# Work from behind the attention chunks moved between their steps, and the value product in quarters of the array

## The chip, the cores and the metric

The kernel runs on one core of one Trainium2 chip. The metric is the device time of one execution in microseconds. TensorE (PE), VectorE (DVE), ScalarE (ACT), GpSimd (POOL) and SyncE (SP, which here only issues transfers) run side by side and meet at semaphores.

## What is computed

```python
x = L0_attn_x                                  # 2 x 2048 tokens, 256 wide, fp32
h = _layernorm(x) * (1 + ca) + sa              # mod from silu(c) @ wmod
x = x + ga * attention(h, Wqkv, Wout)          # 16 heads of 64, causal window of 128
h = _layernorm(x) * (1 + cb) + sb
x = x + gb * experts(h)                        # 8 experts, top 2 by softmax, 640 rows
...                                            # per expert and choice; 256 -> 1024 -> 256
```

Within the window a query of a block of 128 tokens sees the keys of its own block up to itself and those of the block before that lie behind it: two triangles that together make one full block.

## The kernel before

The 4096 tokens are eight chunks of 512 (four tiles of 128); chunks 0 to 3 are the first batch. A chunk has 16 units, each half of a pair of heads (two heads, two of the four tiles); in the last chunk (7) the units run over the pairs for the first two tiles, then for the last two. `chunk` of each engine walks 16 steps, numbered 4 to 19. In step i, PE issues the scores of unit i (line 637, `scores`; from 16 on that is a unit of the next chunk), the values of unit i-4 (lines 668 and 675, `weighted_values`), the turning of unit i-2 (line 648, `transposes`), and projections of the next chunk (line 600 for queries and keys, 614 for values). DVE merges the two triangles (1109), takes maximum and reciprocal (1113, 1117) and normalises (1121); ACT takes the exponentials (909), copies the turned probabilities out of the bank `pt` (917) and empties the projections (894, 901); POOL splits the triangles into previous and own keys (`split_keys`, 1422 and 1424). The result in the one bank `pv` is written as high and low fp16 halves, by ACT (923) and DVE (1134), once per pair; in the last chunk once per unit (931, 1246).

Score and value products are fp32; each is recorded as two matmuls. Scores work in quarters of the array (64 rows, 64 columns), values in halves (128 rows of keys, 64 columns), the rest on all of it. fp16 products are three matmuls on high and low halves.

The projections write two banks in turn, `gen0` and `gen1`: `chunk_groups` lists all groups of a chunk in order, and `claim` makes PE wait until the group before the previous one has been emptied. Behind the 16 steps stand the four value tiles of the second half of the heads (`projections_after`) and the output projection of the chunk (`project_out`, 691); DVE then adds the result to `x` (`add_attention`, 1142 and 1146).

The second layernorm, the choice of experts and the sending of rows for chunk c-1 (`ROUTE_AT`) run during chunk c: statistics, then scale and shift on POOL (370, 374), packing on ACT (943), the low half on POOL (379), turning by DMA, logits on PE (740), softmax and top 2 on DVE, counts on PE (754), slots on DVE (1206 to 1227), and eight scatters on POOL (1433). SP also copies the last block of keys of each pair for the next chunk by DMA (530; in chunk 0 DVE does it, 1093), clears the slots in the first 110 us (522) and turns normalised rows (535). After chunk 7 come the experts (1603, 1617). All of `x` stays in memory (32 tiles).

```python
    LATE_PACKED = 2016
...
                names = [("qk"[i % 2], (i - LAG) // 2)] + ([("v", 0, v_tiles[i])] if i in v_tiles else [])
...
                return names + projections_after(c) + out_groups
```

## Time and profile before

| | us |
|---|---|
| median of 3 runs | 1151.61 |
| lowest, highest | 1149.98, 1154.63 |
| profiled execution, its own time | 1147.24 |
| its span (first to last instruction) | 1144.4 |
| chunk 0, start to end | 54.4 to 135.4 |
| chunks 1 to 5 | 83.3 each |
| chunks 6 and 7 | 73.7 and 71.0 |
| experts | from 707.4 |

The profiled execution took 2.8 us more than its span, and 4.4 us less than the median of the runs. Busy time of an engine in a stage, set against the stage's length, tells how far it is from setting the pace there; the mean granted TensorE clock over the span is 0.991 of full.

### The profile page before, as it was taken

The numbers are of one execution on the slowest core, as the hardware profiler recorded it, in microseconds if no ns is written. First come the engines' busy times: TensorE is split into PE (matmuls) and PEld (weight loads), VectorE is DVE, ScalarE is ACT, GpSimd is POOL, SyncE is SP. The second block draws the span as 40 slices with busy tenths as digits, with TensorE's granted clock in tenths as the row PEclk, the third lists the DMA queues.
The fourth block names the chain that finished last, engine by engine and source line by source line (L and its number), as shares of the span: only waits on it lengthen the run. The fifth ranks groups of instructions, "written<-read, shape, count | busy, mean of one in ns | idle before, by whom it ended". The sixth has DMA issues, their size and how long they took to land.

```text
span 1144.4 us, 25293 instructions
## 1 busy us (share of the span) xinstructions
PE 1084.4 (95%) x9469; PEld 711.8 (62%) x9469; DVE 750.3 (66%) x1663; ACT 660.5 (58%) x1874; POOL 506.2 (44%) x555
## 2 busy tenths in 40 slices
PE   7999999999999999999998885989999999999996
PEld 4455655655655655655656564756776858585765
DVE  5776586586576585674675784756676766666653
ACT  5677476476476476476473853447474563727461
POOL 2234274365275365355445655434344352525342
PEclk9999999999999999999999998999999999999998
DMA  9744111112021021021031024434345353534000
GB/s 335 151 163 138 40 29 48 38 37 52 27 45 48 24 46 45 24 45 39 24 103 48 5 83 121 92 94 81 109 94 153 97 112 111 112 112 78 23 20 9
DMA packets 140114, 87.41 MB, mean 76 GB/s; under 512 B 96708, under 2 KB 130650, under 8 KB 139868
## 3 DMA queue, kind: packets, MB, share of 16 engines
q1 hardware_dynamic: 129244, 64.29, 21.4%
q0 software_dynamic: 10752, 21.54, 6.6%
q8 instruction: 75, 1.23, 0.5%
q14 instruction: 43, 0.35, 0.1%
HBM read 40.02 MB, written 33.79 MB: 64 GB/s over the span
## 4 chain that ended last, share of the span: by engine, by line
PE 75%; issue 7%; DVE 7%; ACT 6%; POOL 4%; DMA 0%; SPq 0%; POOLq 0%; DVEq 0%; ACTq 0%
PE down L1617 18%; PE up L1603 17%; PE gen L600 10%; PE gen L614 7%; PE gen L691 6%; PE score L637 4%; PE pv L668 4%; PE pt L648 4%; ACT prob L909 4%; PE pv L675 3%; DVE prob L1121 2%; POOL h L370 1%; POOL probT_split L1424 1%; PE gen L699 1%; POOL probT_split L1422 1%
## 5 line engine op out<-in xcount | busy, mean ns | idle before, releaser
L1643 ACT ACTIVATE hid<-up,b1T 128x512 f16<-128x512 f32 (+2 forms) x192 | 124.3, 648 | 182.1 <-PE up L1603 180.3
L1603 PE MATMUL up<-xT,w 128*128 128x512 f16 (+2 forms) x1152 | 212.5, 346 | 10.9 <-issue 10.9
L1617 PE MATMUL down<-w,hid 128*128 128x256 f16 x1920 | 213.7, 274 | 3.2 <-DVE hid L1659 3.2
L1422 POOL TENSOR_SCALAR_AFFINE_SELECT probT_split<-probT 128x512 f32<-128x512 f32 x128 | 102.9, 804 | 250.9 <-ACT probT L917 247.4
L1617 PEld LDWEIGHTS down<-w,hid 128*128 128x128 f16 x1920 | 188.6, 98 | 27.6 <-DVE hid L1659 3.7
L600 PE MATMUL gen<-hT,big 128*128 128x512 f16 x768 | 185.0, 380 | 0.6 <-DVE hT L1371 0.6
L909 ACT ACTIVATE prob<-score,negmax 128x128 f32<-128x128 f32 x512 | 180.7, 375 | 0.7 <-DVE negmax L1113 0.7
L1603 PEld LDWEIGHTS up<-xT,w 128*128 128x128 f16 x1152 | 112.9, 98 | 104.9 <-issue 12.8
L1702 POOL DMA_INDIRECT out<-y,tail x80 | 82.4, 1031 | 206.1 <-DVE y L1687 193.2
L1659 DVE TENSOR_TENSOR hid<-hid 128x512 f16<-128x512 f32 (+2 forms) x192 | 115.2, 606 | 72.4 <-ACT hid L1644 72.0
L917 ACT ACTIVATE probT<-pt 128x512 f32<-128x512 f32 x128 | 76.9, 601 | 99.0 <-PE pt L648 98.8
L1109 DVE COPY_PREDICATED score<-above,score 128x512 f32<-128x512 int32 x112 | 77.5, 692 | 77.3 <-PE score L637 77.2
L1644 ACT ACTIVATE hid<-up,b1T 128x512 f32<-128x512 f32 (+2 forms) x192 | 124.8, 650 | 0.0
L600 PEld LDWEIGHTS gen<-hT,big 128*128 128x128 f16 x768 | 73.8, 98 | 67.7 <-issue 1.2
L637 PE MATMUL score<-k,q 64*64 64x192 f32 (+2 forms) x2048 | 111.0, 330 | 2.6 <-issue 2.2
L909 ACT ACTIVATION_READ_ACCUMULATOR prob<-score,negmax 128x1 f32 x512 | 111.0, 217 | 0.0
L1692 POOL DMA_INDIRECT kept<-out,tail x80 | 86.5, 1081 | 47.6 <-issue 30.0
L1121 DVE TENSOR_TENSOR prob<-prob,rinv 128x512 f32<-128x512 f32 x128 | 103.4, 808 | 0.0
L668 PE MATMUL pv<-probT_split,v 128*64 128x256 f32 x512 | 83.5, 403 | 19.0 <-DVE attn L1134 7.0
L637 PEld LDWEIGHTS score<-k,q 64*64 64x64 f32 x2048 | 64.5, 132 | 53.9 <-issue 51.6
L614 PE MATMUL gen<-big,hT 128*128 128x512 f16 x384 | 89.1, 379 | 2.3 <-DVE logit L1160 1.2
L1424 POOL TENSOR_SCALAR_AFFINE_SELECT probT_split<-probT 128x512 f32<-128x512 f32 x128 | 86.3, 674 | 0.0
(159 smaller groups left out, 1442.4 us busy)
## 6 DMA issues: line engine op xcount, KB each, us to landing
big<-in_L_ffn_W SPq DMA_DIRECT2D x14, 1024.0 KB, 6.9
slot_inputs<-empty_row SPq DMA_DIRECT2D x80, 129.5 KB, 2.3
out<-x SPq DMA_DIRECT2D x7, 512.0 KB, 3.3
x<-in_L_attn_x SPq DMA_DIRECT2D x1, 3072.0 KB, 22.8
k<-k SPq DMA_DIRECT2D x48, 64.0 KB, 1.9
kept<-out,tail POOLq DMA_INDIRECT x80, 3.1
out<-y,tail POOLq DMA_INDIRECT x80, 2.4
x<-in_L_attn_x SPq DMA_DIRECT2D x2, 512.0 KB, 6.9
```

What stands on the lines that cost most here:

```text
L600: mm = pe.matmul(dst[:], wqkv[:, kd, a, col:col + P], hT[:, cn % 2, kd, b, :], start=(n == 0), stop=(n == 5))
L614: mm = pe.matmul(dst[:], hT[:, cn % 2, kd, a, s * P:(s + 1) * P], wqkv[:, kd, b, 2 * INNER + half * 512:2 * INNER + (half + 1) * 512], sta ...
L637: mm = pe.matmul(dst[lo:lo + HALF, 2 * hd + i, first:lo + P + HALF], q[r:r + DH, j, b * P + lo:b * P + lo + HALF], k[r:r + DH, j, b * P + ...
L668: mm = pe.matmul(pv[r:r + DH, 2 * part * P:(2 * part + 2) * P], v[:, 2 * part + 1, h * DH:(h + 1) * DH], probT_split[:, par, 2 * hd:2 * hd ...
L909: mm = act.activation(prob[:, h % 2, b, :], score[h % 2][:, b, P:], ACT.Exp, bias=negmax[:, h % 2, b:b + 1], accum_out=rowsum[:, h % 2, b: ...
L1121: dve.tensor_tensor(prob[:, h % 2], prob[:, h % 2], rinv[:, h % 2, :].unsqueeze(2).to_broadcast([P, TILES, P]), ALU.mult)\
L1422: pool.affine_select(out=probT_split[:, h % 2, :, 1], in_=probT[:, h % 2], pattern=[[0, TILES], [1, P]], compare_op=ALU.is_ge, fill=zero, ...
L1603: mm = pe.matmul(bank, w1[:, par, kd, a, ft * P:(ft + 1) * P], part_rows(e, n, xT[:, par, b * KD + kd, :]), start=(i == 0), stop=(i == 5))
L1617: mm = pe.matmul(down[n][:, s, :], hid[:, ft, a, t * P:(t + 1) * P], w2[:, par, ft, b, :], start=(i == 0), stop=(i == 3 * FT - 1))
L1643: act.activation(part_rows(e, n, hid[:, ft, 0, :]), bank, ACT.Relu, scale=1 / W_SCALE, bias=bias).then_inc(hid_hi, 1)
L1644: act.activation(part_bank(e, n, hid32[:, k_ % 4, :]), bank, ACT.Relu, scale=1 / W_SCALE, bias=bias).then_inc(up_out, 1)
L1659: dve.tensor_tensor(part_rows(e, n, hid[:, ft, 1, :]), part_bank(e, n, hid32[:, k_ % 4, :]), part_rows(e, n, hid[:, ft, 0, :]), ALU.subtra ...
```

## The change

1. **Values in quarters.** In chunks 0 to 6 a value product is no longer made of whole blocks of 128 keys. `half_values` takes the upper 64 keys of a new unit (`high_keys`) and the lower 64 keys of the unit before it (`low_keys`), in turn, and leaves out the 64x64 corners that the window masks. The two go to two banks, `pv0` and `pv1`. The lower half of a unit comes a step later (`LO_AT` 5, `HI_AT` 4). High and low fp16 halves are written per unit, and `attn` has 24 slots of 256 columns in a ring. The last chunk keeps `weighted_values`, on two banks.
2. **The turned probabilities** lose the bank `pt`: they take their turn on `gen0` and `gen1`. ACT copies them straight into `probT_split` (three buffers, `RING`), where POOL splits them in place.
3. **The output projection** of chunk c-1 runs in steps 4, 6, 8 and 11 of chunk c, a tile at a time (`late_out`, `add_tile`), the second half of chunk c's own values in steps 5, 7, 9 and 10. Chunk 6 keeps its output behind its steps.
4. **Routing** moves: statistics to packing of chunk c-1 from steps 4 to 9 to steps 8 to 16 of chunk c, logits to sending into steps 4 to 12 of the chunk after that. The rows that chunk 6 makes ready are chosen and scattered behind its steps (`logits_late`, `counts_late`).
5. **Key copies** are DVE's in all chunks (`keep_keys`).
6. **x** has 24 tiles; chunks 6 and 7 are loaded later into places that are free by then. Expert 0's weights go to other places and are loaded after chunk 6; their splits move from steps 5 to 8 of the last chunk to 7 to 10.

```diff
-    LATE_PACKED = 2016
+    X_PLACE = (2, 3, 0, 1, 4, 5, 2, 3)
+    X_CHUNKS = max(X_PLACE) + 1
+    ATTN_SLOTS = H + PAIRS
+    LATE_PACKED = (ATTN_SLOTS - H) * 4 * P
     EARLY_TILES = 3
+    RING = 3
     EARLY_ROWS = EARLY_TILES * P
...
-            probT_split = sb("probT_split", [P, 2, TILES, 2, P], F32)
+            probT_split = sb("probT_split", [P, RING, TILES, 2, P], F32)
...
-            attn = sb("attn", [P, PAIRS, 2, CHUNK], F16)
+            attn = sb("attn", [P, ATTN_SLOTS, 2, 2 * P], F16)
...
-            pv = ps("pv", [P, CHUNK], F32)
+            pv = [ps(f"pv{i}", [P, CHUNK], F32) for i in range(2)]
...
-                v_tiles = {12: 0, 13: 1, 14: 2, 16: 3}
+                v_tiles = {13: 0, 14: 1, 16: 2, 17: 3}
...
-                return [n for n in v_half(1) if c < LAST and (c != LAST - 1 or n not in LATE_NAMES)]
...
+                return [n for n in v_half(1) if c == LAST - 1 and n not in LATE_NAMES]
...
+            OUT_TILE = {4: 0, 6: 1, 8: 2, 11: 3}
+            SECOND_V = {5: 0, 7: 1, 9: 2, 10: 3}
...
+            ROUTE_AT = {"stats": (8, 13), "rstd": 13, "norm": 14, "scale": 14, "shift": 15, "token": 16, "pack": 16, "low": 16}
+            CHOOSE_AT = {"logits": 4, "softmax": 5, "exp": 5, "top": 6, "counts": 7, "slots": 8, "send": 9, "sent": 13}
...
-            SPLIT_AT = [5, 6, 7, 8]
+            SPLIT_AT = [7, 8, 9, 10]
...
+                    names += [("pt", i)]
+                    if c > 1:
+                        names += ([("logits",)] if i == CHOOSE_AT["logits"] else []) + ([("counts",)] if i == CHOOSE_AT["counts"] else [])
...
+                        names += [("tile", OUT_TILE[i])] if i in OUT_TILE else []
+                        names += [("own v", SECOND_V[i])] if i in SECOND_V else []
+                    names += projections_at(c, i)
...
+                    def transposes(n_unit, c, name):
+                        pe.wait_ge(norm_ready, n_unit + 1)
+                        dst, full = claim(c, name)
...
+                            mm = pe.transpose(dst[:, b * P:(b + 1) * P], prob[:, n_unit % 2, b, :], identf[:])
+                        mm.then_inc(full, 1)
...
+                        at_least(pe, attn_lo, n_unit - 1)
...
+                    def high_keys(c, u, hd, i, cur):
+                        n_unit = H * c + u
+                        j, part = unit_of(c, u)
+                        r, h, b = DH * hd, 2 * j + hd, 2 * part + i
+                        first = HALF * cur
+                        return pe.matmul(pv[n_unit % 2][r:r + DH, i * P + first:(i + 1) * P], v[HALF:, b + cur, h * DH:(h + 1) * DH],
+                                         probT_split[HALF:, n_unit % RING, 2 * hd + i, cur, first:], start=(i == 0 and cur == 0),
+                                         stop=False, skip_group_check=True)
+
+                    def low_keys(c, u, hd, i, cur):
+                        n_unit = H * c + u
+                        j, part = unit_of(c, u)
+                        r, h, b = DH * hd, 2 * j + hd, 2 * part + i
+                        last = P if cur else HALF
+                        return pe.matmul(pv[n_unit % 2][r:r + DH, i * P:i * P + last], v[0:HALF, b + cur, h * DH:(h + 1) * DH],
+                                         probT_split[0:HALF, n_unit % RING, 2 * hd + i, cur, 0:last], start=False,
+                                         stop=(cur == 0), skip_group_check=True)
+
+                    def half_values(c, new, old):
+
+                        if old is not None:
+                            pe.wait_ge(high_done, H * old[0] + old[1] + 1)
+                        if new is not None:
+                            values_there(c, new)
+                        for i in range(2):
+                            for n in range(2):
+                                for hd in range(2):
+                                    if new is not None:
+                                        high = high_keys(c, new, hd, i, n)
+                                    if old is not None:
+                                        low = low_keys(*old, 1 - hd, i, 1 - n)
+                        if new is not None:
+                            high.then_inc(high_done, 1)
+                        if old is not None:
+                            low.then_inc(pv_done, 1)
...
+                    def late_out(c, t):
+                        if c == 0 and t == 0:
+                            pe.wait_ge(split_lo, 8)
+                        pe.wait_ge(attn_lo, H * c + (H - 1 if t < 2 else H))
+                        dst, full = claim(c + 1, ("tile", t))
+                        project_out_tile(c, dst[:, 0:D], t, range(PAIRS)).then_inc(full, 1)
...
+                                scores(c, i)
+                                half_values(c, i - HI_AT, (c, i - LO_AT) if i >= LO_AT else (c - 1, H - 1) if c > 0 else None)
+                            transposes(H * c + i - 2, c, ("pt", i))
+                            if c > 1 and i == CHOOSE_AT["logits"]:
+                                route_logits(c - 1)
+                            if c > 1 and i == CHOOSE_AT["counts"]:
+                                route_counts(c - 1)
+                            if c > 0 and i in OUT_TILE:
+                                late_out(c - 1, OUT_TILE[i])
+                            if c > 0 and i in SECOND_V:
+                                project_v(c - 1, 1, [SECOND_V[i]])
+                            for name in projections_at(c, i):
+                                project(c, name)
+                        if c == LAST - 1:
                             for name in projections_after(c):
                                 project(c, name)
-                            project_out(c)
-                            return
-                        pe.wait_ge(attn_lo, PAIRS * c + H - 1)
+                            route_logits(c)
+                            project_out_pair(c, 0)
+                            route_counts(c)
+                            project_out_pair(c, 1)
...
                     def copy_probT(c, h):
                         u = H * c + h
-                        act.wait_ge(pt_done, u + 1)
-                        at_least(act, prev_ready, u - 1)
-                        act.activation(probT[:, h % 2], pt[:], ACT.Copy).then_inc(probT_ready, 1)
-
-                    def attn_high(c, j):
-                        act.wait_ge(pv_done, H * c + 2 * j + 2)
-                        if j == 0:
-                            at_least(act, x2_ready, 2 * c)
-                        act.activation(attn[:, j, 0, :], pv[:], ACT.Copy).then_inc(attn_hi, 1)
+                        bank, before = turned_in(u)
+                        act.wait_ge(gen_full[bank], before + 1)
+                        at_least(act, pv_done, u - RING + 1)
+                        act.activation(probT_split[:, u % RING, :, 1], gen[bank][:].rearrange("p (a q) -> p a q", q=P), ACT.Copy)\
+                           .then_inc(gen_free[bank], 1)
 
...
+                    def keep_keys(c, j):
+
+                        dve.wait_ge(scores_done, H * c + 2 * j + 2)
+                        dve.tensor_copy(k[:, j, 0:P], k[:, j, CHUNK:]).then_inc(k_halo[j], 1)
 
...
+                    def add_tile(c, t):
+
+                        bank, before = group(c + 1, ("tile", t))
+                        if c == 0 and t == 0:
+                            dve.wait_ge(mod_spread, 16)
+                        at_least(dve, x2_ready, TILES * c + t)
+                        dve.wait_ge(gen_full[bank], before + 1)
+                        dve.scalar_tensor_tensor(gated[:, t % 2, :], gen[bank][:, 0:D], 1 / W_SCALE, modrow[:, batch(c), 0, :],
+                                                 ALU.mult, ALU.mult).then_inc(gen_free[bank], 1)
+                        dve.wait_ge(gen_free[bank], before + 1)
+                        row = x[:, x_at(c) + t, :]
+                        dve.tensor_tensor(row, row, gated[:, t % 2, :], ALU.add).then_inc(x2_ready, 1)
 
                     def route_tokens(r):
                         c, t0, nt, rows_out = route_round(r)
...
                         for i in STEPS:
-                            if i >= 6 and i % 2 == 0 and not last:
-                                attn_low(c, (i - 6) // 2)
-                            if not first and not last and i == at["softmax"]:
+                            if i > LO_AT:
+                                attn_low_part(c, i - LO_AT - 1)
+                            elif c > 0:
+                                attn_low_part(c - 1, H + i - LO_AT - 1)
+                            if c > 0 and i == LO_AT:
+                                keep_v(c - 1, 1)
+                            if c > 0 and i - 1 in OUT_TILE:
+                                add_tile(c - 1, OUT_TILE[i - 1])
+                            if c > 1 and i == CHOOSE_AT["softmax"]:
+                                route_softmax(c - 1)
+                            if c > 1 and i == CHOOSE_AT["slots"]:
+                                route_slots(c - 1)
...
+                        pool.wait_ge(gen_free[bank], before + 1)
+                        whole, own = probT_split[:, u % RING, :, 1], probT_split[:, u % RING, :, 0]
+                        pool.affine_select(out=own, in_=whole, pattern=[[0, TILES], [-1, P]],
+                                           compare_op=ALU.is_gt, fill=zero, base=0, channel_multiplier=1).then_inc(prev_ready, 1)
+                        pool.affine_select(out=whole, in_=whole, pattern=[[0, TILES], [1, P]],
                                            compare_op=ALU.is_ge, fill=zero, base=0, channel_multiplier=-1).then_inc(cur_ready, 1)
```

PE in the first step of chunk 2. Before:

```order
L637 MATMUL score0<-k,q 64x192 x8
L668 MATMUL pv<-probT_split,v 64x256 x2
L675 MATMUL pv<-probT_split,v 64x128 x4
L648 MATMUL pt<-identf,prob 128x128 x4
L600 MATMUL gen0<-hT,big 128x512 x6
```

and now, from the second half of the value product on (line 703 is `high_keys`, 712 `low_keys`, 755 an output tile, 813 the logits, 683 the turning):

```order
L703 MATMUL pv0<-probT_split,v 64x128
L712 MATMUL pv1<-probT_split,v 64x128
L703 MATMUL pv0<-probT_split,v 64x128
L712 MATMUL pv1<-probT_split,v 64x128
L703 MATMUL pv0<-probT_split,v 64x64
L712 MATMUL pv1<-probT_split,v 64x64
L703 MATMUL pv0<-probT_split,v 64x64
L712 MATMUL pv1<-probT_split,v 64x64
L683 MATMUL gen0<-identf,prob 128x128 x4
L813 MATMUL gen1<-gate16,h2T 128x8 x24
L755 MATMUL gen0<-wout,attn 128x256 x24
L636 MATMUL gen1<-hT,big 128x512 x6
```

The value product has become 16 small products between the scores and the turning, and two groups, logits and an output tile, stand between the turning and the projection. The turned probabilities and the output tile are on the same bank, `gen0`, the logits and the projection on `gen1`.

DVE in steps 9 and 10 of a middle chunk (1080 and 1180 are `ln_shift`). Before:

```order
L1109 COPY_PREDICATED score1<-above,score1 128x4x128
L1117 RECIPROCAL rinv<-rowsum 128x4
L1113 TENSOR_REDUCE negmax<-score1 128x4
L1121 TENSOR_TENSOR prob<-prob,rinv 128x512
L1080 SCALAR_TENSOR_TENSOR xn<-xn,rstd0,kept 128x256 x2
L1134 TENSOR_TENSOR attn<-pv,attn 128x512
L1109 COPY_PREDICATED score0<-above,score0 128x4x128
L1117 RECIPROCAL rinv<-rowsum 128x4
L1113 TENSOR_REDUCE negmax<-score0 128x4
L1121 TENSOR_TENSOR prob<-prob,rinv 128x512
L1080 SCALAR_TENSOR_TENSOR xn<-xn,rstd0,kept 128x256 x2
```

and now, from the first instruction of step 9:

```order
L1355 TENSOR_TENSOR attn<-pv1,attn 128x256
L1251 SCALAR_TENSOR_TENSOR gated<-gen1,modrow 128x256
L1255 TENSOR_TENSOR x<-x,gated 128x256
L1209 COPY_PREDICATED score1<-above,score1 128x4x128
L1217 RECIPROCAL rinv<-rowsum 128x4
L1213 TENSOR_REDUCE negmax<-score1 128x4
L1221 TENSOR_TENSOR prob<-prob,rinv 128x512
L1180 SCALAR_TENSOR_TENSOR xn<-xn,rstd0,kept 128x256 x2
L1355 TENSOR_TENSOR attn<-pv0,attn 128x256
L1193 COPY k<-k 128x128
L1209 COPY_PREDICATED score0<-above,score0 128x4x128
```

The low half comes in every step and for one unit, ahead of it all; behind it stand the residual of an output tile (1251, 1255) or a key copy (1193), both ahead of the merge.

POOL at the end of chunk 6. Before, the scatters stood between the pairs of selects of that chunk's last four steps:

```order
L1422 AFFINE_SELECT probT_split<-probT 128x4x128
L1424 AFFINE_SELECT probT_split<-probT 128x4x128
L1433 DMA slot_inputs<-packed,send 10240x518 x2
L1422 AFFINE_SELECT probT_split<-probT 128x4x128
L1424 AFFINE_SELECT probT_split<-probT 128x4x128
```

and now all eight stand behind the last pair, ahead of the selects of chunk 7's second unit:

```order
L1550 AFFINE_SELECT probT_split<-probT_split 128x4x128
L1552 AFFINE_SELECT probT_split<-probT_split 128x4x128
L1561 DMA slot_inputs<-packed,send 10240x518 x8
L1550 AFFINE_SELECT probT_split<-probT_split 128x4x128
L1552 AFFINE_SELECT probT_split<-probT_split 128x4x128
```

## Rows read from the trace of the kernel before

**Rows 1.** the page, part 1: busy us (share of the span) x instructions

```profile
PE 1084.4 (95%) x9469; PEld 711.8 (62%) x9469; DVE 750.3 (66%) x1663; ACT 660.5 (58%) x1874; POOL 506.2 (44%) x555
```

**Rows 2.** busy time, chunks 0, 2, 6, 7: length; PE, PEld, DVE, ACT, POOL; clock

```profile
54.40:135.40 81.00, 79.72 (x755) 48.75 (x754) 50.06 (x105) 52.37 (x186) 26.38 (x35) 1.00 0.37 120
218.70:302.00 83.30, 81.61 (x791) 50.21 (x790) 56.05 (x137) 51.36 (x179) 41.80 (x48) 1.00 0.17 40
551.90:625.60 73.70, 68.75 (x731) 44.71 (x731) 50.24 (x121) 44.81 (x168) 38.65 (x45) 1.00 0.20 62
625.60:696.60 71.00, 61.68 (x676) 41.75 (x675) 54.33 (x152) 44.85 (x147) 41.16 (x43) 1.00 0.16 53
```

**Rows 3.** PE in order of time, one plain step; start, us, what

```profile
226.15 0.88 PE L637 MATMUL score<-k,q 64*64 64x192 f32 x16
226.96 0.65 PE L668 MATMUL pv<-probT_split,v 128*64 128x256 f32 x4
227.44 0.61 PE L675 MATMUL pv<-probT_split,v 128*64 128x128 f32 x8
227.98 0.66 PE L648 MATMUL pt<-identf,prob 128*128 128x128 f32 x4
228.47 1.46 PE L600 MATMUL gen<-hT,big 128*128 128x512 f16 x6
```

**Rows 4.** what PE waited for, whole run: us, times, longest

```profile
PE pv L668 <- DVE attn L1134: 7.0, 13, 1.3
PE pv L668 <- POOL probT_split L1424: 6.9, 14, 1.4
...
PE pv L668 <- DVE attn L1246: 2.1, 2, 1.3
```

**Rows 5.** score instructions alone, the first 0.03 us of a step

```profile
222.43:222.46 0.03, 0.02 (x4) 0.03 (x4) 1.00 0.96 341
```

**Rows 6.** PE in order of time, the logits of chunk 2

```profile
251.93 0.75 PE L740 MATMUL gen<-gate,h2T 128*128 128x8 f16 x24
252.53 1.45 PE L600 MATMUL gen<-hT,big 128*128 128x512 f16 x6
```

**Rows 7.** PE in order of time, behind chunk 1

```profile
202.97 5.34 PE L614 MATMUL gen<-big,hT 128*128 128x512 f16 x24
208.15 10.64 PE L691 MATMUL gen<-wout,attn 128*128 128x256 f16 x96
```

**Rows 8.** ACT in order of time, the same plain step

```profile
228.03 0.22 ACT L909 ACTIVATION_READ_ACCUMULATOR prob<-score,negmax 128x1 f32 x1
228.68 0.60 ACT L917 ACTIVATE probT<-pt 128x512 f32<-128x512 f32 x1 [0.42 <-PE pt L648]
```

**Rows 9.** groups of instructions by line and shape: us, mean ns, idle before

```profile
L1246 DVE TENSOR_TENSOR attn<-pv,attn 128x256 f16<-128x256 f32 x16 | 6.7, 418 | 2.3 <-ACT attn L931 2.3
...
L931 ACT ACTIVATE attn<-pv 128x256 f16<-128x256 f32 x16 | 6.3, 391 | 21.0 <-PE pv L675 21.0
...
L1093 DVE COPY k<-k 128x128 f32<-128x128 f32 x8 | 3.9, 484 | 0.0
```

**Rows 10.** DVE in order of time, the same plain step

```profile
228.95 0.68 DVE L1121 TENSOR_TENSOR prob<-prob,rinv 128x512 f32<-128x512 f32 x1
```

**Rows 11.** POOL, and below it ACT, in order of time, chunk 2

```profile
231.02 2.37 POOL L370 TENSOR_TENSOR h<-h,modrow 128x1024 f32<-128x1024 f32 x1 [4.02 <-DVE h L237]
...
240.65 1.05 ACT L943 ACTIVATE packed<-h 128x1024 f16<-128x1024 f32 x1
```

**Rows 12.** SP in order of time, end of the clearing of the slots

```profile
111.80 6.17 SPq L535 DMA_TRANSPOSE hT<-h  x4
```

**Rows 13.** POOL in order of time, two scatters of chunk 6

```profile
606.86 0.99 POOL L1433 DMA_INDIRECT slot_inputs<-packed,send  x1 [0.17 <-issue]
608.15 1.42 POOL L1433 DMA_INDIRECT slot_inputs<-packed,send  x1 [0.30 <-PE pv L675]
```

**Rows 14.** DMA issues by line; KB each, median us from issue to landing

```profile
kept<-in_L_ffn_W SPq DMA_DIRECT2D x1, 1024.0 KB, 7.8
```

605 lines of the change are left out of this document (316 added, 289 removed).

## The prediction

> **What bounds the kernel now.** I read the page first: PE is busy 95% of the span [rows 1]. Then the busy time by stage [rows 2]: a full chunk of attention lasts 83.3 us, of which PE works 81.6, DVE 56 and ACT 51. So in a chunk PE's own work is the length and 1.7 us is waiting; the chunk before last waits 5.0 us of 73.7, the last 9.3 of 71.0, the first 1.3 of 81.0. Chunks 0 to 6 together wait 15.2 us (four further full chunks wait 1.68, 1.66, 2.29 and 1.66). Everything after the last chunk (from 696.6 us, 448 us) is experts, which the change leaves as they are but for two loads. Then PE's order of time in one plain step [rows 3]: scores 0.81, values 1.02 (0.48 and 0.54), turning 0.49, a projection 1.39, in all 3.71 us with no gap. Last, what PE waited for [rows 4]: in the whole run VectorE's low half for 7.0 us and POOL's split keys for 6.9.
>
> **The values.** One score matmul streams 192 fp32 columns in each quarter of the array; four start within 0.03 us [rows 5], so quarters run side by side. A projection of 512 fp16 columns takes 0.217 us (1.30 for six). A score product sends each quarter 4 x 192 columns, by that pace (fp32 at two passes for each of its two recorded matmuls) 0.64 us, and lasts 0.81: 0.17 goes into emptying and refilling the array where the tile shape changes. Today's values stream 0.86 in each half (512 columns in four passes) and last 1.02, so 0.16 goes there again. The new form computes 3/4 of the area in 64x64 pieces, 384 columns per quarter: 0.64. Its tile shape is that of the scores, so scores and values together pay 0.17 once: 0.64 + 0.64 + 0.17 = 1.45 for today's 1.83, a gain of 0.38 per unit. It is made in chunks 0 to 6, 112 units: **-42.6 us**. The lone half at the end of chunk 6 costs 0.5. A plain step becomes 3.33. Bounds: no row has a 64-column piece. If it takes as long as one of 128 (0.107), four per unit cost 0.21 more, 24 us in all; nearest below is streaming alone, with no switch at all, 0.17 better per unit, excluded since the turning has another shape. I take proportional time, since rows of 512, 192 and 128 columns all follow it.
> The logits show another limit: 24 matmuls of 8 columns take 0.60 us, 0.025 each [rows 6]. At that pace the 32 recorded matmuls of a unit need 0.80, not 0.64: 18 us of the gain goes. I take the other, because four in 0.03 us go to different quarters, as here. The Trainium skill (TensorE: Matmul & The Clock Gate, "Wait — 56ns, not 53.3ns?") says that starts never come closer than about 25 ns; by that rule the result would be some 1146, by the score row 1128. The score rows contradict it across quarters.
>
> **The spread work.** The 24 value and 96 output matmuls behind a chunk last 5.2 and 10.6 us [rows 7]; their number is unchanged, now 2.66 per output tile and 1.30 per value tile between steps. For PE this is nothing. It matters for the others, whose slack must be found per step. With T the start of a step's scores:
> ACT: the last exponential (228.03 and 0.22) ends at T+2.1, T being 226.15 here [rows 8]; the high half of 256 columns (0.39 [rows 9]) makes 2.5, the copy of the turned keys (0.60) 3.0. The turned keys now share the two banks of the projections: the third group of a step wants the bank of this copy. After turning (T+1.94) and a group of 1.30 that is T+3.24: no wait.
> DVE: normalising starts at T+2.8 and ends at 3.5 [rows 10], then the low half of 256 columns (0.42 [rows 9]) ends at 3.9; PE wants it at 3.33+0.7 = 4.0. It just fits, and any step with further DVE work behind the softmax is also one with a group more, but for small excesses, 0.3 per chunk. DVE does a low half per unit where it did one twice as wide per pair, and 48 key copies of 0.48 mean [rows 9], ahead of the merge, where it waits for scores anyway; even the 0.64 that a copy beside POOL's select takes fits. Cover gone, they would cost up to 0.64 x 48 = 31 us, kept as an end. SP loses 48 copies' issues, which nothing waited for.
> Step 4 (chunks 2 to 6): the second group is the logits, 0.6, so the output tile waits 0.4 for the key copy, and the projection behind it wants the logits' bank, which DVE empties behind the residual of that very tile. Tile over at T+5.7, signal, two adds of 0.42 and 0.18: T+6.9, 1.3 late. Sum 1.7.
> Step 7: counts of 0.36 in second place: 0.7.
> Step 16: normalising rows ends at T14+4.7, POOL's scale 2.37 [rows 11], the selects 1.4, shift as long as the scale, all in a chain: T14+10.9 = T16+2.9; pack 1.05 [rows 11], copy 0.6: T16+4.6 for a wish of 3.24, 1.3. ACT stands in its queue with the key copy behind the pack.
> Chunk 0 ends at about 54.4+58.8+1 = 114; the turned rows of chunk 2 are issued by SP from 111.8 to 118.0, after the clearing of the slots [rows 12], and land at 120; wanted after the first output tile at 119: 1.5.
> So waits: chunk 0 1.0; chunk 1 1.3+0.3+1.5 = 3.1; chunks 2 to 5 4.0 each, 16. In chunk 6 steps 14 to 19 have almost no projections, PE's work is 13 us, while POOL's chain (norm 4.7, scale 2.4, shift 2.4, low 2.4, five pairs of selects 7.0, values 0.7) takes 19.6: 6.6, and 2.4 of steps 4 and 7. Together 29.1, for 15.2 now: **+13.9**.
>
> **Last chunk.** The eight scatters of chunk 6's rows now stand behind its counts: slots some 1.9 after them (ten small DVE operations), 8 x 1.29 (start to start [rows 13]), landing some 2, selects 1.4: 15.7; PE comes to that unit after 5.6 (outputs), 5.8 and 0.8: 12.2. **+3.5**. Step 14's turning wants the bank of the early output, emptied only behind that step's softmax: +2.6. Two value banks take away the two low-half waits of line 1246, -2.1 [rows 4]. The late loads of expert 0's weights (two of 1 MB, one 7.8 us to landing now [rows 14]) begin about 2 us into the chunk and are wanted 17 us in: 0. From loading 1 MB less at the start I take 0; VectorE alone waits for it.
>
> **Sum.** -42.6 + 0.5 + 13.9 + 4.0 = -24.2. The profiled execution took 1147.2 (span 1144.4 and 2.8 around it), so 1123; the median of the runs is 4.4 above it, 1151.6 less 24 = **1128**. A measurement of this kernel can tell 0.5% (5.8 us) from no change.
>
> **Rivals.**
> *A, small pieces are slow.* At the start to start time of the logits 18 us more, at the time of 128 columns 24: 1146 to 1152. For: no row has such a piece, and each brings its own weights. Against: [rows 5].
> *B, the waits are milder.* My steps add the latest signal each time. Today's five full chunks wait only 1.7 to 2.3 although ACT is as close behind. If 2 to 3 of 4 us vanish per chunk, 14 to 18 us less: 1112 (1106 to 1118).
> *C, slower: the shared bank ring.* Place: the eight value tiles per chunk that are the third or second group, wanting the bank of the key copy. It is done 0.24 us ahead of the wish. If ACT is 1.1 late there (a pack does this once already), each waits 0.9: 8 x 6 x 0.9 = 43: 1171. It decides, against today, from 0.5 a tile, a copy 0.75 late. Against: ACT works 51 us of a 79 us chunk.
> *D, the halves don't run together,* the change doesn't do what it says: high and low keys of two units in series, 1.28 instead of 0.64: 72 us more, of which some 20 swallow other waits: 1180. Against: the score rows use both row halves at once, each with its own bank, as here.
>
> **Numbers.** Forecast (1118 to 1140) 0.47, B 0.24, A 0.14, C 0.09, D 0.06. Range 1106 to 1150: it takes in forecast and B, two thirds of A and a little of C; about 0.17 lies above, 0.03 below. Faster: forecast, B and 0.05 of A, 0.76. Same: 0.07 of A and 0.02 of C, 0.09. Slower: 0.02 of A, 0.07 of C, 0.06 of D, 0.15.
>
> **What would show it.** The values of a step should last 0.64 to 0.7 from the scores' end to the turning, with 64-column pieces 0.055 apart in a quarter; 0.8 or more is A, 1.3 is D. A full chunk should last about 79 us, with PE waits before the output tile and the projection of step 4, before the value tile of step 16, and one of 3 to 4 us early in the last chunk. PE waiting for ACT's key copy in most steps is C; a chunk under 77 is B. The experts' 437 us should stand. Wrong it would be most of all if a plain step isn't 3.3 us long.

## The result and the profile after

The changed kernel takes **1159.45 us** (median of 7 runs, 1156.38 to 1161.55) where the kernel before takes 1151.61 (7 runs, 1149.69 to 1154.63): a ratio of 1.0064, 95% interval 1.0048 to 1.0081. Forecast was 1128, range 1106 to 1150. It is slower by 0.64%, and outside the range. The profiled execution took 1161.3 us, its span is 1159.6; against the 1144.4 of before it has 15.2 us too many where I had worked out 24.2 too few. So 39.4 us are to be found. By the medians the miss is 31.5 (1159.45 for 1128). The other 7.9 lie between the two traces: that of before took 1147.24 us, less than any of its seven runs here (1149.69 the lowest), that of the changed kernel 1161.33, near the top of its own. It isn't on record whether the trace of before comes from the chip of these runs.

First the busy time by stage of the changed kernel (length; then PE, PEld, DVE, ACT, POOL; clock), for chunks 0 to 7 and the experts. A stage begins with the scores of its step 4, the experts with the first product of expert 0:

```profile
55.00:117.10 62.10, 59.53 (x937) 38.70 (x936) 48.16 (x108) 47.87 (x180) 27.33 (x34) 1.00 0.50 152
117.10:194.60 77.50, 75.62 (x1075) 51.13 (x1074) 56.47 (x128) 51.13 (x186) 36.44 (x41) 1.00 0.12 30
194.60:277.60 83.00, 78.38 (x1115) 52.47 (x1114) 60.29 (x159) 51.69 (x187) 44.01 (x49) 1.00 0.15 40
277.60:362.20 84.60, 77.81 (x1111) 52.23 (x1110) 63.35 (x160) 51.58 (x187) 43.88 (x49) 1.00 0.14 33
362.20:444.90 82.70, 77.73 (x1111) 51.89 (x1110) 60.97 (x164) 51.71 (x187) 44.07 (x49) 1.00 0.14 34
444.90:527.40 82.50, 78.00 (x1115) 52.47 (x1114) 56.85 (x147) 51.34 (x187) 42.21 (x47) 1.00 0.16 34
527.40:620.00 92.60, 83.00 (x1229) 60.20 (x1228) 60.07 (x177) 50.15 (x191) 41.53 (x47) 1.00 0.10 24
620.00:716.90 96.90, 68.55 (x676) 43.49 (x676) 59.49 (x164) 45.44 (x148) 50.86 (x58) 0.87 0.25 78
716.90:1159.60 442.70, 424.84 (x3097) 303.48 (x3097) 273.25 (x499) 231.99 (x414) 171.97 (x164) 0.98 0.36 88
```

They answer to [rows 2]. Work has moved across the borders of the chunks, so only sums compare: chunks 0 to 6 last 565.0 us for 571.2 (6.2 less; I had 28.2 less), the last one 96.9 for 81.8 (15.1 more; I had 4.0 more), the experts 442.7 for 437.0 (5.7 more; I had none), and the start is 0.6 later.

One plain step, PE in order of time, for [rows 3] (lines 673 scores, 703 and 712 values, 683 turning, 636 projection):

```profile
255.65 0.88 PE L673 MATMUL score<-k,q 64*64 64x192 f32 x16
256.35 0.27 PE L712 MATMUL pv<-probT_split,v 64*64 64x128 f32 x1
...
256.98 0.22 PE L712 MATMUL pv<-probT_split,v 64*64 64x64 f32 x1
257.12 0.66 PE L683 MATMUL gen<-identf,prob 128*128 128x128 f32 x4
257.62 1.46 PE L636 MATMUL gen<-hT,big 128*128 128x512 f16 x6
259.01 0.39 PE L673 MATMUL score<-k,q 64*64 64x192 f32 x4
```

Scores and values start 1.47 us ahead of the turning, and the step lasts 3.36: 1.45 and 3.33 were forecast. The skew does what it was made for. What PE waited for, whole run, for [rows 4]:

```profile
PE pv L703 <- DVE attn L1355: 8.8, 10, 2.2
PE gen L650 <- ACT probT_split L1011: 7.4, 12, 0.9
PE gen L636 <- DVE logit L1269: 6.2, 5, 1.2
PE pv L703 <- POOL probT_split L1552: 5.7, 8, 1.7
PE gen L636 <- ACT probT_split L1011: 4.6, 1, 4.6
```

### The profile page after: what moved, and what is told of

Read it like the earlier page. It is cut to its first block, busy times and chain, and to the rows that moved or that the text cites. A ratio compares the mean times of both kernels' runs of the same rounds, so it can differ in the third digit from the quotient of the medians.

```text
span 1159.6 us, 29936 instructions
## 1 busy us (share of the span) xinstructions
PE 1068.9 (92%) x11709; PEld 729.5 (63%) x11709; DVE 775.9 (67%) x1791; ACT 663.7 (57%) x1930; POOL 514.8 (44%) x555
## 4 chain that ended last, share of the span: by engine, by line
PE 75%; DVE 7%; issue 6%; ACT 6%; POOL 4%; DMA 1%; another core or an unknown queue 0%; SPq 0%; DVEq 0%; ACTq 0%; POOLq 0%
PE down L1760 17%; PE up L1746 17%; PE gen L636 12%; PE gen L755 7%; PE gen L650 6%; PE score L673 5%; PE gen L683 4%; ACT prob L1002 3%; PE pv L712 3%; PE pv L703 2%; DVE prob L1221 1%; POOL h L404 1%; POOL h L408 1%; ACT probT_split L1011 1%; DVE xn L1172 1%
## 5 line engine op out<-in xcount | busy, mean ns | idle before, releaser
L1786 ACT ACTIVATE hid<-up,b1T 128x512 f16<-128x512 f32 (+2 forms) x192 | 121.8, 634 | 185.0 <-PE up L1746 169.1
L1550 POOL TENSOR_SCALAR_AFFINE_SELECT probT_split<-probT_split 128x512 f32<-128x512 f32 x128 | 110.0, 859 | 264.8 <-ACT probT_split L1011 259.7
L1746 PE MATMUL up<-xT,w 128*128 128x512 f16 (+2 forms) x1152 | 214.9, 348 | 12.8 <-issue 12.8
L636 PE MATMUL gen<-hT,big 128*128 128x512 f16 x768 | 188.3, 385 | 11.4 <-DVE logit L1269 6.2
L1787 ACT ACTIVATE hid<-up,b1T 128x512 f32<-128x512 f32 (+2 forms) x192 | 121.9, 635 | 0.0
L703 PE MATMUL pv<-probT_split,v 64*64 64x64 f32 (+1 forms) x1792 | 96.7, 245 | 14.8 <-DVE attn L1355 8.8
L703 PEld LDWEIGHTS pv<-probT_split,v 64*64 64x64 f32 x1792 | 92.1, 133 | 25.8 <-issue 24.3
L650 PE MATMUL gen<-big,hT 128*128 128x512 f16 x384 | 93.4, 383 | 9.2 <-ACT probT_split L1011 7.4
L712 PE MATMUL pv<-probT_split,v 64*64 64x128 f32 (+1 forms) x1792 | 99.5, 246 | 0.2
L985 ACT ACTIVATE q<-gen 128x512 f32<-128x512 f32 x64 | 38.2, 597 | 98.9 <-PE gen L636 98.0
```

The source lines that it names most:

```text
L636: mm = pe.matmul(dst[:], wqkv[:, kd, a, col:col + P], hT[:, cn % 2, kd, b, :], start=(n == 0), stop=(n == 5))
L650: mm = pe.matmul(dst[:], hT[:, cn % 2, kd, a, s * P:(s + 1) * P], wqkv[:, kd, b, 2 * INNER + half * 512:2 * INNER + (half + 1) * 512], sta ...
L703: return pe.matmul(pv[n_unit % 2][r:r + DH, i * P + first:(i + 1) * P], v[HALF:, b + cur, h * DH:(h + 1) * DH], probT_split[HALF:, n_unit ...
L712: return pe.matmul(pv[n_unit % 2][r:r + DH, i * P:i * P + last], v[0:HALF, b + cur, h * DH:(h + 1) * DH], probT_split[0:HALF, n_unit % RIN ...
L1550: pool.affine_select(out=own, in_=whole, pattern=[[0, TILES], [-1, P]], compare_op=ALU.is_gt, fill=zero, base=0, channel_multiplier=1).the ...
L1746: mm = pe.matmul(bank, w1[:, par, kd, a, ft * P:(ft + 1) * P], part_rows(e, n, xT[:, par, b * KD + kd, :]), start=(i == 0), stop=(i == 5))
```

## The experiments

Kernels of one block ran on one chip, each beside the kernel before; the blocks ran on four different chips, so I compare ratios, and inside a block times. The first two blocks may be compared by their times as well, since before took 1148.22 us in one and 1148.23 in the other, and neither shows the late signals told of next. The trace of the changed kernel showed, in steps 9 to 13 of chunks 2 to 6 and at the start of chunk 7, that those who wait for TensorE start up to 1.5 us (at the end 4.6) behind the modelled end of its products. Scatters are issued in just those stretches. The scatters were my first suspect.

### First block: scatters, loads, the skew

**e1_no_scatters**: no scatters in rounds 1 to 6 (the waits for them go too).

```
-    scatter(c - 1, [i - pick["send"]])
-    if c > 1 and i == pick["sent"]:
-        pool.wait_ge(sent, 16 * TILES * K * (c - 1))
...
-    scatter(c, range(TILES))
-    pool.wait_ge(sent, 16 * TILES * K * c)
...
```

> The changed kernel with the 48 row scatters of rounds 1 to 6 left out (their rows never reach the experts' slots; TensorE's work is the same). In the changed kernel TensorE's signals come up to 1.5 us after the modelled end of its products in steps 9 to 13 of chunks 2 to 6, in the stretches in which POOL issues scatters, and 4 to 5 us late at the start of chunk 7, where eight scatters stand in a row; then the clock falls for 13.65 us. Theory S (scatters issued beside the scores and values hold TensorE's path): steps 9 to 13 lose their 2.4 to 3.2 us per chunk, the start of chunk 7 its 6.8, the half clock behind it goes, in all 22 to 30 us less than the changed kernel: 1130 to 1138. Rival R (what is late in these steps is VectorE's and ScalarE's other work, scatters only stand beside it): at most 3 us less in chunks 2 to 6, 1150 or more.

**e2_spread**: chunk 6's eight scatters go from POOL's part of chunk 6 into that of chunk 7, in pairs; the wait for their landing, and the writing of chunk 7's token numbers, go to step 8.

```
-    scatter(c, range(TILES))
-    pool.wait_ge(sent, 16 * TILES * K * c)
...
     for i in STEPS:
+        if i == 8:
+            pool.wait_ge(sent, 16 * TILES * K * (c - 1))
         if i - 3 < H:
             split_keys(c, i - 3)
+        if i < 8:
+            scatter(c - 1, [i - 4])
```

> The changed kernel with the eight scatters of chunk 6's rows not in one row ahead of chunk 7's first selects, but in pairs behind the selects of steps 4 to 7 of chunk 7, and the wait for their landing in step 8. Theory S: the 4.6 us wait in the first projection pair and most of the 6.8 us of step 4 go, the clock does not fall there, a pair costs 1 us: 6 to 12 us less than the changed kernel, 1147 to 1153. Rival L (the two 1 MB loads of expert 0's weights, which start in the same microsecond, hold TensorE): the stall at the start of chunk 7 stays, 1157 to 1161.

**e3_whole_values**: `half_values` calls the old `weighted_values(c, new)` and returns.

> The changed kernel with the old form of the values (128 rows at once, one unit per step) in chunks 0 to 6, everything else as it is. If a skewed unit saves the 0.35 us that the steps without a wait show (3.71 to 3.36), 112 units cost 39 us less what the waits give back (they are of the order of 7 us a chunk, and a longer TensorE step lets others catch up): 1175 to 1190. If the skewed form is itself what makes scatters hold TensorE (rival K: small pieces are the ones that stall), the late signals of steps 9 to 13 are gone with it and the time is 1160 to 1170.

**e4_late_loads**: `sp.wait_ge(scores_done, H * LAST + 6)` ahead of `load_expert`.

> The changed kernel with the loads of expert 0's weights held back until the scores of chunk 7's step 5 are done. Rival L: the stall at the start of chunk 7 goes with them, and with it the half clock: 6 to 10 us less, 1149 to 1153. Theory S: the stall is that of the eight scatters, the signal of the first scores is late before any load is issued, so the stall stays: 1157 to 1161.

Measured (before: 1148.22): e1 1137.61, 0.9904 (0.9887 to 0.9920); e2 1138.26, 0.9903 (0.9882 to 0.9924); e3 1179.64, 1.0280 (1.0257 to 1.0303); e4 1147.34, 0.9989 (0.9975 to 1.0002). e3, at 1175 to 1190 as forecast, shows that the skew is worth some 30 us (how far that is exact stands below). But no trace of this block has the late signals, not even e2, e3 and e4 with the same scatters in the same steps. So a control was due before e1, e2 and e4 could be read.

### Second block: the control, and two waits

**c0_after** is the changed kernel itself.

> The changed kernel once more, unchanged, as the control for the trace: in its first profile TensorE's signals came up to 1.5 us late in steps 9 to 13 of chunks 2 to 6, and the kernels with only chunk 6's scatters spread (1138.3) or only the late loads (1147.3) showed none of that with the same scatters in the same steps. If the late signals belong to the kernel, they are here again and chunks 2, 4 and 5 last 82.5 to 83.0 us. If they belong to that one execution, the chunks last 79.8 to 80.8 us, as in those two kernels, and the time is 1150 to 1156 where before is 1148 to 1151.

**e5_logits_first** (on e2): VectorE's `route_softmax(c - 1)` ahead of `add_tile(...)` in step 5.

> The kernel with chunk 6's scatters spread (1138.3), and VectorE empties the bank of the logits in step 5 ahead of the residual of output tile 0, instead of behind it. My reading of step 4: the projection behind the tile waits 1.25 us for that bank, in five chunks. If so, 5 x 1.25 = 6 us less, 1131 to 1134, and the wait on line 1269 is gone. Rival: the projection is followed by a turning that then waits for the tile's bank or for the softmax instead, nothing gained, 1137 to 1139.

**e6_pack_last** (on e5): ScalarE's `route_pack(c)` in step 16 behind the loop that copies that step's projections.

> The kernel e5_logits_first, and ScalarE's packing of routed rows in step 16 stands behind the copies of that step's turned keys and projections instead of ahead of them. If the 1.5 us that step 16 loses is ScalarE standing in its queue at the pack, six chunks give back 1.1 to 1.5 us each: 6 to 9 us less than e5_logits_first. If it is only moved to step 17 or 18 (exponentials and the merge behind a later low half on POOL), 0 to 2 us less.

**e7_double_copies** (on e2):

```
     dve.wait_ge(scores_done, H * c + 2 * j + 2)
+    dve.tensor_copy(spare[:, j % 2, :], k[:, j, CHUNK:])
     dve.tensor_copy(k[:, j, 0:P], k[:, j, CHUNK:]).then_inc(k_halo[j], 1)
```

> The kernel with chunk 6's scatters spread (1138.3), with a second copy of the same size (128 columns of keys into a spare tile) ahead of each of VectorE's 56 copies of old keys. If the copies are covered, as I took (cost 0), a second one of 0.34 us costs at most 3 us in all. If each costs its own time on the path, 48 x 0.34 = 16 us and more: 1154 or above.

Measured (before: 1148.23): c0 1146.79, **0.9982** (0.9967 to 0.9997); e5 1131.46, 0.9845 (0.9832 to 0.9858); e6 1125.15, **0.9811** (0.9791 to 0.9831); e7 1153.97, 1.0053 (1.0039 to 1.0068). The same kernel that was 0.64% slower is here 0.18% faster. Chunk 0 starts at 55.9 us. Chunks 2 to 7 and the experts:

```profile
195.60:276.40 80.80, 77.02 (x1115) 52.10 (x1114) 61.12 (x158) 51.26 (x187) 43.80 (x49) 1.00 0.17 41
276.40:359.90 83.50, 78.23 (x1111) 52.90 (x1110) 63.92 (x160) 51.26 (x187) 43.87 (x49) 0.98 0.15 34
359.90:440.60 80.70, 76.77 (x1115) 51.61 (x1114) 61.78 (x165) 51.37 (x187) 43.69 (x49) 1.00 0.15 35
440.60:520.40 79.80, 76.78 (x1115) 52.13 (x1114) 57.32 (x147) 51.04 (x187) 42.81 (x47) 1.00 0.14 35
520.40:612.80 92.40, 83.48 (x1229) 61.39 (x1228) 60.19 (x177) 49.81 (x191) 42.57 (x47) 0.98 0.10 24
612.80:707.30 94.50, 63.99 (x676) 42.51 (x676) 59.02 (x164) 45.33 (x148) 50.51 (x58) 0.90 0.26 80
707.30:1145.00 437.70, 422.99 (x3097) 303.13 (x3097) 273.97 (x499) 230.53 (x414) 172.49 (x164) 0.98 0.37 89
```

Chunks 0 and 1, which issue no scatters beside their steps, last 62.2 and 77.5 us: the same as in the first measurement. Chunks 2 to 6 are together 8.2 us shorter (417.2 for 425.4). The control loses 3.4 us in chunks 3 and 6 to two stretches of half clock that the first measurement doesn't have (both chunks at 1.00 there), so the late signals themselves cost more than these 8.2, by an estimate from the two clocks some 11 to 12. The rest of the difference lies in chunk 7 (2.4) and the experts (5.0). The stretch that makes the 8.2, in order of time, chunk 2, step 10; first the first measurement:

```profile
230.17 0.88 PE L673 MATMUL score<-k,q 64*64 64x192 f32 x16
230.17 0.99 POOL L1561 DMA_INDIRECT slot_inputs<-packed,send  x1 [0.16 <-issue]
...
231.51 0.70 DVE L1209 COPY_PREDICATED score<-above,score 128x512 f32<-128x512 int32 x1 [0.76 <-PE score L673]
...
233.26 0.38 ACT L1020 ACTIVATE attn<-pv 128x256 f16<-128x256 f32 x1 [0.99 <-PE pv L712]
```

and the control:

```profile
230.91 0.88 PE L673 MATMUL score<-k,q 64*64 64x192 f32 x16
...
231.16 0.99 POOL L1561 DMA_INDIRECT slot_inputs<-packed,send  x1 [0.16 <-issue]
...
231.86 0.70 DVE L1209 COPY_PREDICATED score<-above,score 128x512 f32<-128x512 int32 x1
...
232.88 0.40 ACT L1020 ACTIVATE attn<-pv 128x256 f16<-128x256 f32 x1
```

VectorE gets the scores 1.34 us behind their start instead of 0.95, ScalarE the values 3.09 instead of 1.97, with the same scatter of 0.99 us beside them. Taken over 190 to 530 us, where VectorE waits for scores some 40 to 50 times (31 in before), its merge starts more than 1.1 us behind the start of the scores (0.95 is the median) 10 times in the first measurement and never in the control, nor in any trace of the first two blocks or in the one trace of before.

e4 equals the control within 0.6 us (ratios 0.9989 and 0.9982). It does not clear the loads, though: the scores that it waits for are done at some 620 us, when the scatters have still not landed, and TensorE then waits 7.8 us. The loads now start in the same microsecond as the last scatter, and its landing takes 5.44 us. What happens in the changed kernel, the control shows (POOL, SP and PE, in order of time):

```profile
610.46 1.10 POOL L1561 DMA_INDIRECT slot_inputs<-packed,send  x1 [16.00 <-DVE send L1336]
...
615.44 1.00 SPq L119 DMA_DIRECT2D kept<-in_L_ffn_W  x1
...
619.54 0.97 POOL L1561 DMA_INDIRECT slot_inputs<-packed,send  x1 [0.30 <-issue]
625.27 0.63 POOL L1550 TENSOR_SCALAR_AFFINE_SELECT probT_split<-probT_split 128x512 f32<-128x512 f32 x1 [4.75 <-DMA slot_inputs<-packed,send]
...
626.58 1.12 PE L741 MATMUL pv<-probT_split,v 128*64 128x256 f32 x4 [7.12 <-POOL probT_split L1550]
```

and its DMA issues from 606 to 631 us (KB each, median us to landing):

```profile
kept<-in_L_ffn_W SPq DMA_DIRECT2D x1, 1024.0 KB, 10.9
...
slot_inputs<-packed,send POOLq DMA_INDIRECT x8, 5.8
```

Eight scatters in a row, then 4.75 us until the last has landed among the two loads (the second takes 10.9 us, [rows 14] had 7.8), then the selects: TensorE waits 7.1 us, from 619.5 us on. At some 620.6 the granted clock falls to half, 1.2 GHz, and stays there to 630.8, 4 us beyond the wait (0.67 is the mean of the whole step):

```profile
612.80:618.60 5.80, 5.07 (x49) 2.80 (x48) 5.42 (x15) 2.29 (x5) 4.27 (x6) 1.00 0.65 177
618.60:634.00 15.40, 7.54 (x55) 4.35 (x59) 4.10 (x9) 3.94 (x16) 8.85 (x11) 0.67 0.45 157
```

The second step costs 9.6 us more than the one ahead of it (in the kernel before both last 5.8), 7.1 by the wait and 2.5 by the clock. In e2 the wait is gone, chunk 7 lasts 86.6 us for 94.5, and that is nearly all of e2's gain (8.5); in e1, with no scatters of round 6 at all, it lasts 87.9. Rival L, the loads alone, falls: e2 leaves them where they are, and in e1, with the loads and no scatters, TensorE doesn't wait there at all (the second load lands in 9.0 us). That the loads lengthen the last scatter's landing is likely but not shown by itself: in before, with no loads and the scatters in pairs, POOL waits 1.61 us for it, and no run has eight in a row without loads.

e5 and e6 hit the waits that they were made for. Before e5 the line `L1269` stood at 6.2 us in the waits of TensorE; with it, it is gone, and five chunks are some 1.4 us shorter each: 6.8 us. e6 gives 6.3 more. e7 costs 15.7 us over e2, and not evenly: in chunks 1 and 2 (3.9 and 4.1 us longer than in e2) nearly all of it comes from what happens in step 16. TensorE loses it in step 17, which lasts 9.1 us for 4.7. Chunk 2 of e7, VectorE and POOL in order of time:

```profile
262.82 0.32 DVE L1194 COPY spare<-k 128x128 f32<-128x128 f32 x1
263.03 2.35 POOL L409 TENSOR_TENSOR h<-h,modrow 128x1024 f32<-128x1024 f32 x1
263.06 2.41 DVE L1195 COPY k<-k 128x128 f32<-128x128 f32 x1
...
265.39 0.68 DVE L1211 COPY_PREDICATED score<-above,score 128x512 f32<-128x512 int32 x1
...
266.56 2.06 POOL L414 TENSOR_TENSOR packed<-h,packed 128x1024 f16<-128x1024 f32 x1
266.72 2.45 DVE L1223 TENSOR_TENSOR prob<-prob,rinv 128x512 f32<-128x512 f32 x1
```

The second copy starts 0.03 us behind POOL's `h<-h,modrow` and ends 0.09 behind it: 2.41 us for 0.32. The Trainium skill (SBUF — State Buffer, "Who interferes with whom") says that VectorE and GpSimd share a pair of SBUF ports as a lock, and that the one that issues second is blocked for the other's whole instruction; these rows agree (2.41 beside 2.35, 2.45 beside 2.06). The changed kernel has such places already. A residual (1255) beside POOL's `h<-xn,h` takes 2.15 us in each of chunks 1 to 5, and TensorE doesn't wait for it. Chunk 3 has one that counts, the masking of the first block of a batch; all of that line, in the control (min/median/max ns):

```profile
L1206 DVE COPY_PREDICATED score<-above,no_prev x16: 420/434/2607, 24.2 to 414.8; 128x256 f32<-128x256 int32 x16
```

Behind it the token numbers (1260) are held as well, 2.03 us beside POOL's low half, and TensorE waits 2.16 us for VectorE's low half where it waits 0.78 in chunk 2. This and the 1.7 us of half clock behind that wait are why chunk 3 is 2.7 us longer than chunks 2 and 4; in the first measurement, without the half clock, it is 1.6 and 1.9. e3 meets the same lock in steps 16 and 17 of its chunks 1, 2, 3 and 5, so its 32.9 us above the control (1179.64 less 1146.79) aren't the skew alone; what the whole values give back in waits goes the other way.

### Third and fourth block: which chip, which copy

**c1_after** is the changed kernel; **e8_no_copies**, **e9_norm_later** and **e10_counts_behind** are e6 with one edit each: copies of one column in chunks 1 to 6 (`w = P if c == 0 else 1`), `LN_NEXT = 17`, and `route_counts` behind `project_v` in step 7.

> The changed kernel, unchanged, a third time. First measurement: 1.0064 of before, its trace with late signals beside the scatters of steps 9 to 13; second: 0.9982, its trace without them. If the late signals come with a chip or an execution and not with the kernel, this one shows either the one pair or the other, 1.006 with chunks of 82.5 to 83 us or 0.998 with chunks of 80 to 81, and nothing between.

> The kernel e6_pack_last (1125.1), with VectorE's copies of old keys in chunks 1 to 6 cut from 128 columns to 1 (the scores then read keys that aren't theirs in the rest). A second copy cost 15.7 us, nearly all of it in step 17, where VectorE's merge came to stand behind POOL's 2.35 us operation. If that is a threshold that the first copy does not reach in this kernel, leaving it out gains at most 4 us, 1121 to 1125. If every copy is on the path with its time, 48 x 0.25 = 12 us: 1113.

> The kernel e6_pack_last (1125.1), with VectorE's statistics and rows of the chunk after next one step later (steps 17 and 18 for 16 and 17). TensorE's values of steps 17 and 18 wait 0.6 and 1.2 us for VectorE's low half in chunks 1 to 4, behind exactly these 2.0 and 1.8 us. If they are what is late, 4 x 1 us go: 1120 to 1123. If the waits only move by a step: 1124 to 1127.

> The kernel e6_pack_last (1125.1), and the counts of step 7 stand behind that step's value tile instead of ahead of it. The counts last 0.94 there, of which 0.45 is the wait for ScalarE's copy of the turned keys (it is the second group of its step, 0.35 long, and the third wants that bank). Behind the tile nothing is waited for: 5 x 0.5 = 2.5 us less, 1121.5 to 1124. Rival: the next turning then waits for VectorE to empty the counts' bank: nothing gained or 1 us lost.

Measured (before: 1151.39): c1 1158.02, **1.0059** (1.0038 to 1.0080); e8 1141.51, 0.9910 (0.9886 to 0.9935); e9 1146.35, 0.9961 (0.9944 to 0.9977); e10 1140.20, 0.9913 (0.9886 to 0.9939). c1 repeats the first measurement, late signals included (chunks 2 and 4: 83.0 and 82.6 us), and so have the other three. e9, forecast to gain 1 us a chunk, is 5 to 6 us above its neighbours; its forecast falls. e8 and e10 can't be read against e6 of another chip, so they ran again with it, and e1 with them.

> The changed kernel with the 48 scatters of rounds 1 to 6 left out, once more, beside the next three on one chip. On a chip that shows TensorE's late signals beside scatters, the late signals of steps 9 to 13 must be gone here if the scatters make them: chunks 2 and 4 then last 80.8 and 80.6 us, as on the chips without late signals, and 83 us if they come from anything else in these steps. Ratio to before 0.990 on either chip.

> The kernel e6_pack_last again. It gave 0.9811 on a chip without late signals. With late signals beside scatters five chunks are 1.5 to 2.5 us longer and the ratio is 0.988 to 0.991; without them 0.981 again. In either case it is the base beside which the key copies and the counts are to be read on one chip.

> The kernel e6_pack_last with VectorE's copies of old keys in chunks 1 to 6 cut to one column, once more on the chip of e6b_pack_last. If the first copy is covered (my cost of 0), it is within 4 us of e6b_pack_last; if each copy costs its time, 12 us below.

> The kernel e6_pack_last with the counts of step 7 behind the value tile, once more on the chip of e6b_pack_last: 1 to 3 us below it if the counts' wait for ScalarE's key copy was on the path, at or above it if VectorE empties the counts' bank too late.

Measured (before: 1149.40): e1b 1136.40, 0.9893 (0.9871 to 0.9915); e6b 1137.38, 0.9898 (0.9881 to 0.9914); e8b 1134.64, 0.9868 (0.9851 to 0.9884); e10b 1136.81, 0.9892 (0.9874 to 0.9910). Chunks 2 and 4 of e1b, without scatters:

```profile
194.90:275.70 80.80, 77.02 (x1115) 52.10 (x1114) 60.34 (x158) 51.26 (x187) 36.25 (x41) 1.00 0.12 28
357.80:438.40 80.60, 76.70 (x1111) 51.57 (x1110) 60.99 (x164) 51.38 (x187) 36.38 (x41) 1.00 0.12 22
```

of e6b, on the same chip, with them:

```profile
195.40:276.50 81.10, 77.89 (x1111) 52.53 (x1110) 59.96 (x158) 51.79 (x187) 44.48 (x49) 1.00 0.16 41
357.70:438.60 80.90, 77.75 (x1113) 51.78 (x1113) 60.79 (x164) 51.81 (x187) 44.64 (x49) 1.00 0.15 35
```

and of e6 on the other chip:

```profile
194.70:273.90 79.20, 76.89 (x1111) 52.12 (x1110) 60.95 (x158) 51.36 (x187) 44.36 (x49) 1.00 0.19 42
353.10:432.20 79.10, 76.66 (x1111) 51.62 (x1110) 61.71 (x164) 51.51 (x187) 44.24 (x49) 1.00 0.16 36
```

The same e6 is 1.9 and 1.8 us a chunk longer on this chip, and its trace has the late signals (by the count above 11, and 10 to 13 in every other trace of the third and fourth block that has scatters; e1b has none). The changed kernel without scatters has none there, and its chunks last what they do on the chips without them (80.8 and 80.7 in the control). So the late signals need the scatters, and they come in only some of the measurements: with the first, on the chips of blocks three and four, and not on those of one and two. Each block is one chip at one time, so that it is the chip and not the hour is likely, not shown. e8b is 2.7 us below e6b: what the key copies of chunks 1 to 6 cost in all but their one column. e10b equals e6b.

**The best version** that ran is e6_pack_last: the change with chunk 6's scatters spread, the logits' bank emptied first, and the pack last. It is 0.9811 of before on a chip without late signals, where the changed kernel has 0.9982, and 0.9898 on one with them; there the changed kernel wasn't run, on the other such chip it has 1.0059.

## Why the prediction was wrong

39.4 us too optimistic by the spans. Against the control, which has no late signals and whose span is 1145.0 for the 1144.4 of before, the miss is 24.8. Two terms failed in both: TensorE's own work in chunks 0 to 6 (513.9 forecast, 527.5 measured) and chunk 6's scatters (3.5 forecast, 9.6 measured). The rest stands between two measurements of the same kernel, and the forecast had no term for it. By steps, the first part against the control:

- **The values.** Right in kind, and nearly in size: 0.35 us per unit instead of 0.38, 39.2 for 42.6. **3.4 us.** Rival A fell: the 32 small matmuls start within 0.63 us. The Trainium skill's rule that starts never come closer than some 25 ns (TensorE: Matmul & The Clock Gate, "Wait — 56ns, not 53.3ns?") does not hold across quarters. Rival D fell too: the halves start side by side.
- **TensorE's waits in chunks 0 to 6.** Forecast 29.1; in the control they are 29.1 by the trace as well, and that is luck, for the parts don't agree (556.9 us of length; the four largest: VectorE's low half 8.7, ScalarE's key copy 6.8, the logits' bank 6.2, POOL's selects 5.8). Step 4's 1.3 was 1.25, and e5 gave it back; chunk 6's POOL chain, forecast as 6.6, cost 4.6 in three waits. Step 16's 1.3 was 0.9, and the late turned rows of chunk 2 (1.5) didn't happen. For "small excesses, 0.3 per chunk" VectorE's low half took 8.7 us in nine waits. The forecast had it that a step with further VectorE work behind the softmax also has a group more on TensorE. In chunks 1, 2 and 4 that further work is longer than the group, here chunk 2 of the control:

```profile
267.39 2.42 DVE L1172 SCALAR_TENSOR_TENSOR xn<-x,meanvar,kept 128x256 f32<-128x256 f32 x4
...
270.30 0.29 PE L703 MATMUL pv<-probT_split,v 64*64 64x128 f32 x1 [0.78 <-DVE attn L1355]
```

  The low half stands behind these four. In chunk 3, and in one of the three waits of chunk 0, it is the hold by POOL that makes it late.
- **The step that failed first: "with no gap" for the rest.** I took PE's busy time as 556.0 (571.2 less the waits of 15.2) less 42.1, so 513.9. It is 527.5 in the control, 13.6 more. 3.4 is the line above, about 3.4 is half clock in chunks 3 and 6 (mean 0.98 in the two rows: 3.4 us of half speed in each), and the remaining 7 goes with the stops: the projection of step 4 waits 1.25 and comes 1.41 late, the values of step 16 wait 0.21 and come 0.38 late. I counted each wait by its length. In the control the values that wait reach the turning mostly 0.23 us later than 1.48 and the wait explain, in before 0.07 later. With 38 stops that gives 6 to 9 us, an estimate; what TensorE does in these tenths the traces don't say.
- **The scatters beside the steps.** The forecast has no price for moving them. In the first measurement chunks 2 to 6 are 8.2 us longer than in the control. No row of before hinted at it: in its trace the scatters stand at the same spacing, beside scores and values too, and delay nothing. But that is one execution, faster than all seven runs of the first measurement; whether before has late signals on the chips that show them, no trace tells.
- **The last chunk: 15.1 for 4.0.** The term for chunk 6's scatters was 3.5. Its parts: 8 x 1.29 held; the landing was 4.75 instead of 2, beside the loads that I priced at 0 by themselves; and the wait (7.1) brought the clock down (2.5), which I didn't price at all. That is 9.6 for 3.5 in the control; 3.1 more are the rest of the chunk, of which the waits apart from the 7.1 grew by 2.5 (11.8 for 9.3; the bank of the early output cost 2.1 for 2.6, and the two low-half waits went as forecast), and 2.4 come on top in the first measurement.
- **"The experts' 437 us should stand."** 437.7 in the control, 442.7 in the first measurement, 440.9 in c1. Stretches of half clock don't explain it, since before has as many there (in sum some 7 us lost in either trace, an estimate from the granted clock). TensorE works 424.8 us of it for 421.9; the cause stays open.
- **The key copies at 0.** 2.7 us in all (e8b). Too low, and small beside the rest; doubling them cost 15.7, within the bound of 31.

The sum against the control: 3.4 (values) + 10.5 (the rest of chunks 0 to 6) + 8.7 (last chunk) + 0.7 (experts) + 1.5 (start) = 24.8. The sum for the first measurement: 3.4 (values) + 10.5 (the rest of chunks 0 to 6 in the control) + 8.2 (late signals, less the half clock that the control alone has) + 11.1 (last chunk) + 5.7 (experts) + 0.6 (start) = 39.5, for 39.4 by the spans.

The chances failed as well. Every case but C and D assumed that the attention chunks shrink as a sum of steps. Rival B, milder waits, had 0.24 for a remark on today's slack; a rival "each step is as forecast, and the seams between chunks and between engines eat it" wasn't on the list, and it is what happened.

## What to carry to other kernels

Price a moved burst of transfers with what else uses the queues in the same microseconds, and with what the clock does behind the wait that it makes: here 3.5 us became 9.6, and spreading the burst gave 7.9 back. When VectorE gets work that fits by tenths, look for POOL's long operations within those tenths: the same 0.32 us copy costs little in most steps and lasts 2.4 in one. Look as well for what VectorE itself has to do between. And where a result is within a per cent, measure it on a second chip before a cause is named: this kernel is 0.6% slower on one and 0.2% faster on another.
